# An 8-head edge attention on one core: the tensor engine's semaphores raised by drain instructions instead of by the matmuls

## The chip, the cores and the metric

The kernel runs on one core of a Trainium2 chip. The metric is the device time in microseconds (us) of one execution of the whole program. The engines are called PE (tensor), DVE (vector), ACT (scalar), POOL (GpSimd) and SP (sync, which here only issues DMAs).

## The reference

A two-layer graph transformer over 6,250 nodes of 256 features and 206,250 directed edges sorted by destination. Each layer adds a graph part and a dense mixing part, then a mixture-of-experts part. The change lies in the graph part of the first layer, an 8-head softmax attention over the edges that end in each node:

```
q = (h @ Wq + bq).reshape(n, HD, HEADS) * scaling
k = (h @ Wk + bk).reshape(n, HD, HEADS)
v = (h @ Wv + bv).reshape(n, HD, HEADS)
s = einsum('edh,edh->eh', q[rows], k[cols])
m = segment_max(s, rows)
e = exp(s - m[rows])
z = segment_sum(e, rows)
attn = e / z[rows]
out = segment_sum(attn[:, None, :] * v[cols], rows)
```

Everything else in the two layers (projections, mixing, experts, the second layer's edge sums) is as before and runs in stages of its own, with a barrier between two stages.

## The kernel before, in words

`edge_attention` works on edges in steps of 256: two tiles of 128 edges (one edge to a partition) whose destinations lie in one window of 128 nodes. There are 856 steps (`NSTEP`), taken in chunks of 8 (`CS`), so 107 chunks (`NCH`) of 16 tiles. `chunks` is a hardware loop whose body holds two chunks, one for each of two buffers `s`. All queues are written out by hand, engine by engine, and each engine goes through its list in order; semaphores join them. `at(eng, sem, c, per, i)` waits until `sem` has reached `c * per + i + 1`; with a loop register for the value it issues a register operation (L43), the wait (L45) and a no-op.

What a chunk i needs, in the order of the data:

- POOL gathers key and value rows of the 16 tiles (`gather`, L928, an indirect DMA for each tile) into `kv[:, s]`; each group of four tiles waits for `agg_ps` of chunk i - 2.
- ACT builds one-hot matrices: `oht` (L941, L946) and `oh` (L957, L964).
- PE `expand` (L1033): four matmuls of 128 x 256 for a group of four tiles spread the query rows of the windows over the edges, into one half of `psQ`; the group raises `q_ps`. DVE `product` (L1111) multiplies by the keys, `over_heads` (L1116) reduces to scores.
- PE `turn_scores` (L1040) transposes the scores (`st_ps`); DVE `scans` (L1126 to L1128); PE M1 (L1067, `m1_ps`); DVE `carries` (L1134 to L1137); PE M2 (L1072, `m2_ps`); DVE `maxima` (L1141 to L1150); ACT exponentials (L1002, L1003); PE transposes the weights into `psP` (L1079, `p_ps`); DVE `rescale` (L1155) and PE FAC (L1081, L1082, `fac_ps`); DVE `correct` (L1172) scales the first accumulator row.
- DVE `weigh` (L1165) multiplies the values by the weights, four tiles at a time; PE `sums` adds them up: for each step u two matmuls with the one-hot weights (L1048, L1049) and a third with the identity that adds the accumulator row (L1053), which raises `agg_ps`. ACT `keep` (L968) copies the result back to the accumulator row (`acc_done`). Step u's first matmul waits for `keep` of u - 2 (the half of `psA`), its third for `keep` of u - 1 (the row).

PE's own order in the body for chunk i is: M1; steps 4 and 5 of chunk i - 1; M2; steps 6 and 7 of chunk i - 1; `expand` group 1 of chunk i + 1; the transpose into `psP`; FAC; `expand` group 2; steps 0 and 1 of chunk i; `expand` group 3; steps 2 and 3; `turn_scores` of chunk i + 1; `expand` group 0 of chunk i + 2. `windows` (L885) loads registers with the numbers of the windows, five times a chunk on PE. In the profile each fp32 matmul stands as two records (x2 in the timeline) and so does its weight load; the 128 x 128 transposes are one.

Of the kernel before, what the change touches and what calls it, by code (L numbers as in the profile page):

```python
# [26 lines left out]
P = 128  # L27
N = 6250
C = 256
# [571 lines left out]
def at(eng, sem, c, per, i):  # L601

    v = c * per + i + 1
    if not isinstance(v, int) or v > 0:
        wait_reg(eng, sem, v)
# [214 lines left out]
def edge_attention(nc, k, w):  # L820
# [5 lines left out]
    with ExitStack() as c:  # L826
# [3 lines left out]
        oht = sb("oht", [P, 2, CT * P])  # L830
# [6 lines left out]
        S = sb("S", [P, CT, HEADS])  # L837
        FL = sb("FL", [P, 2 * P])
        F, L = FL[:, 0:P], FL[:, P:2 * P]
        R, E = (sb(n, [P, P]) for n in ("R", "E"))  # L840
        rhs1 = sb("rhs1", [P, 2, CT])
        xs, ys, rhs2 = sb("xs", [HEADS, CT + 1]), sb("ys", [HEADS, CT + 1]), sb("rhs2", [HEADS, 2, CT])
        junk, inr = sb("junk", [P, 2, CT]), sb("inr", [P, 2])
        fd, fx, gm, ohrow = sb("fd", [HEADS, 1]), sb("fx", [HEADS, 1]), sb("gm", [HEADS, HEADS]), sb("ohrow", [HEADS, P])
        psQ = c.enter_context(nc.psum_tensor("e_psQ", [P, 2, 4, C], F32))
        psA = c.enter_context(nc.psum_tensor("e_psA", [P, 2, 512], F32))
        psX = c.enter_context(nc.psum_tensor("e_psX", [P, 512], F32))
        psP = c.enter_context(nc.psum_tensor("e_psP", [P, 512], F32))
        ST, M1, M2, FAC = psX[:, 0:P], psX[0:HEADS, P:P + 2 * CT], psX[:, 2 * P:2 * P + 2 * CT], psX[:, 3 * P:3 * P + HEADS]
# [4 lines left out]
        q_ps, st_ps, m1_ps, m2_ps, p_ps, fac_ps, agg_ps = (sem(n) for n in (  # L854
            "q_ps", "st_ps", "m1_ps", "m2_ps", "p_ps", "fac_ps", "agg_ps"))
# [6 lines left out]
        acc = k.QA  # L862

        def chunks(eng, body):

            body(0, 0)
            body(1, 1)
            with eng.Fori(1, (NCH - 3) // 2) as j:
                body(2 * j, 0)
                body(2 * j + 1, 1)  # L870
            for i in range((NCH - 3) // 2 * 2, NCH):
                body(i, i % 2)

        def first_of(i):
            return isinstance(i, int) and i == 0

        def last_of(i):
            return isinstance(i, int) and i == NCH - 1

        def inside(i):  # L880
            return not isinstance(i, int) or i < NCH

        def windows(engine, first, n, table=k.step_i):

            return nc.values_load_multi_w_load_instructions(  # L885
                table[0:1, bass.ds(first, n)], engines=[engine], min_val=0, max_val=NT + 1 if table is k.step_r else NT - 1,
                skip_runtime_bounds_check_because="the tables hold the window of each step, min(count, NT - 1), or NT + 1")[1]

        @block.sync
        def _(sp):  # L890
            sp.dma_start(acc[:, 1:NT + 1, 0:C], k.Q.rearrange("(t p) c -> p t c", p=P)).then_inc(q_in, 16)

            def ahead(i, s):
                at(sp, oht_abs, i - 2, 2, 1)
                sp.dma_start(relb[:, s, :], k.REL.rearrange("s e -> (s e)")[bass.ds(i * CT * P, CT * P)].partition_broadcast(P))\
                    .then_inc(rel_in[s], 16)

            def behind(i, s):
                at(sp, x3_done, i - 2, 1, 0)
                sp.dma_start(t3[:, s, :], k.T3D[bass.ds(i * CT, CT), :].unsqueeze(1).to_broadcast([CT, HEADS, TW])).then_inc(t3_in[s], 16)  # L900
                sp.dma_start(flg[:, s].rearrange("p t f -> p (t f)"),
                             k.FLG.rearrange("t f -> (t f)")[bass.ds(i * CT * 4, (CT + 1) * 4)].partition_broadcast(HEADS)).then_inc(flg_in[s], 16)
            ahead(0, 0)
            ahead(1, 1)
            behind(0, 0)

            def body(i, s):
                if inside(i + 2):
                    ahead(i + 2, s)
                if inside(i + 1):  # L910
                    behind(i + 1, 1 - s)
            chunks(sp, body)
# [114 lines left out]
        @block.tensor  # L1027
        def _(pe):
            def expand(i, s, g, b):
                at(pe, oht_done, i, 2, g // 2)  # L1030
                at(pe, mul_done, i, 4, g - 2)
                for t in range(4 * g, 4 * g + 4):
                    last = pe.matmul(psQ[:, g % 2, t % 4, :], oht[:, s, t * P:(t + 1) * P],  # L1033
                                     acc[:, bass.ds(b[t // 2 % 4] + 1, 1), 0:C].rearrange("p a n -> p (a n)"), start=True, stop=True)
                last.then_inc(q_ps, 1)

            def turn_scores(i):
                at(pe, s_done, i, 4, 3)
                at(pe, x3_done, i - 1, 1, 0)
                pe.transpose(ST, S[:].rearrange("p t h -> p (t h)"), k.ident[:]).then_inc(st_ps, 1)  # L1040

            def sums(i, s, g, r):
                at(pe, pv_done, i, 4, g)
                if g % 2 == 0:
                    at(pe, oh_done, i, 2, g // 2)
                for u in (2 * g, 2 * g + 1):
                    at(pe, acc_done, i, CS, u - 2)
                    pe.matmul(psA[:, u % 2, 0:VW], oh[:, s, 2 * u, :], kv[:, s, 2 * u, C:KW], start=True, stop=False)  # L1048
                    pe.matmul(psA[:, u % 2, 0:VW], oh[:, s, 2 * u + 1, :], kv[:, s, 2 * u + 1, C:KW], start=False, stop=False)  # L1049
                    at(pe, acc_done, i, CS, u - 1)  # L1050
                    if u == 0:
                        at(pe, fac_done, i, 1, 0)
                    pe.matmul(psA[:, u % 2, 0:VW], k.ident[:], acc[:, bass.ds(r[u % 4], 1), :].rearrange("p a n -> p (a n)"),  # L1053
                              start=False, stop=True).then_inc(agg_ps, 1)
            pe.wait_ge(q_in, 16)
            pe.wait_ge(zeroed, 3)
            for g in range(4):
                if g % 2 == 0:
                    b = windows(mybir.EngineType.PE, 2 * g, 4)
                expand(0, 0, g, b)  # L1060
            turn_scores(0)
            expand(1, 1, 0, windows(mybir.EngineType.PE, CS, 4))

            def body(i, s):
                more = inside(i + 1)
                at(pe, x1_done, i, 1, 0)
                pe.matmul(M1, k.selh[:], rhs1[:].rearrange("p a t -> p (a t)"), start=True, stop=True).then_inc(m1_ps, 1)  # L1067
                if not first_of(i):
                    r = windows(mybir.EngineType.PE, i * CS - 4, 4, k.step_r)
                    sums(i - 1, 1 - s, 2, r)  # L1070
                at(pe, x2_done, i, 1, 0)
                pe.matmul(M2, k.selT[:], rhs2[:].rearrange("p a t -> p (a t)"), start=True, stop=True).then_inc(m2_ps, 1)  # L1072
                if not first_of(i):
                    sums(i - 1, 1 - s, 3, r)
                if more:
                    expand(i + 1, 1 - s, 1, windows(mybir.EngineType.PE, i * CS + CS, 4))
                at(pe, exp_done, i, 1, 0)
                at(pe, pv_done, i - 1, 4, 3)
                pe.transpose(psP[:, 0:P], E[:], k.ident[:]).then_inc(p_ps, 1)  # L1079
                at(pe, g_done, i, 1, 0)  # L1080
                pe.matmul(FAC, k.ones[0:1, :], k.ones[0:1, 0:HEADS], start=True, stop=False)  # L1081
                pe.matmul(FAC, ohrow[:], gm[:], start=False, stop=True).then_inc(fac_ps, 1)  # L1082
                if more:
                    b = windows(mybir.EngineType.PE, i * CS + CS + 4, 4)
                    expand(i + 1, 1 - s, 2, b)
                r = windows(mybir.EngineType.PE, i * CS, 4, k.step_r)
                sums(i, s, 0, r)
                if more:
                    expand(i + 1, 1 - s, 3, b)
                sums(i, s, 1, r)  # L1090
                if more:
                    turn_scores(i + 1)
                if inside(i + 2):
                    expand(i + 2, s, 0, windows(mybir.EngineType.PE, i * CS + 2 * CS, 4))
                if last_of(i):
                    for g in range(2, 4):
                        sums(i, s, g, windows(mybir.EngineType.PE, i * CS + g // 2 * 4, 4, k.step_r))
            chunks(pe, body)

        @block.vector  # L1100
# [2242 lines left out]
```

## Time and profile before

| | us |
|---|---|
| time, median of 3 runs | 9517.41 |
| lowest and highest run | 9510.29, 9522.67 |
| profiled execution, its span (first to last instruction; it is all that is given of this execution's own time) | 11525.6 |
| the edge attention of the change, in the profiled execution | 3305 (600 to 3905 us) |

The profiled execution took 2,008 us more than the median of the timed runs, and nothing tells how this is shared out over the stages. The page gives busy times of engines, the stretch windows give the same for one stage with the granted clock of PE and the busy share of the 16 DMA engines, and the timeline gives instructions with the idle time before them in brackets.

### The profile page before, as it was taken

The page shows a single profiled execution, that of the slowest core. Times are in us where ns is not written, and L with a number is a line of the kernel's source. Part 1 is how long each engine was busy: PE and PEld are TensorE (multiplying, and loading weights), DVE is VectorE, ACT ScalarE, POOL GpSimd, SP SyncE. Part 2 cuts the span into 40 slices and gives each one's busy share as a digit, 9 for nine tenths or more (in the row PEclk, how much of TensorE's full clock was granted, in tenths as well). Part 3 has the DMA queues.
Part 4 walks back from the last instruction along what each step waited for, and adds up shares of the span by engine and source line. Part 5 has one row for each costly group of instructions (what it writes and reads, how often), then busy time and mean ns, then how long its engine had stood idle before and what let it go on. Part 6 is the DMA issues. An engine that isn't in the chain of part 4 may idle for free. (4 is left out here: it accounts for less than half of the span.)

```text
span 11525.6 us, 128623 instructions
## 1 busy us (share of the span) xinstructions
PE 7080.4 (61%) x28206; PEld 5254.5 (46%) x28207; DVE 4671.1 (41%) x10764; ACT 3053.2 (26%) x7326; POOL 5829.5 (51%) x6292
## 2 busy tenths in 40 slices
PE   6757777777777877775777455554444624344342
PEld 3345555555555676665765234333333413223231
DVE  6755566656565565554555111111111302111125
ACT  2244444444444311111111133332222201011010
POOL 1145455545554206666664466666666354545541
PEclk9889999989999987767787666666666767677675
DMA  3255555555555332224444333333223311111114
GB/s 99 85 189 165 161 163 166 163 160 164 162 164 163 117 111 68 66 66 130 140 137 123 91 103 103 104 98 88 85 86 88 97 24 35 29 30 32 29 31 145
DMA packets 656102, 1227.40 MB, mean 106 GB/s; under 512 B 164894, under 2 KB 408018, under 8 KB 655797
## 3 DMA queue, kind: packets, MB, share of 16 engines
q0 software_dynamic: 300272, 718.30, 22.8%
q1 hardware_dynamic: 328103, 467.66, 12.9%
q10 hardware_dynamic: 27580, 39.79, 0.9%
q8 instruction: 54, 0.88, 0.0%
q14 instruction: 93, 0.76, 0.0%
HBM read 1088.28 MB, written 145.05 MB: 107 GB/s over the span
## 5 line engine op out<-in xcount | busy, mean ns | idle before, releaser
L928 POOL DMA_INDIRECT e_kv<-KV,e_idx x1712 | 1622.4, 948 | 987.2 <-issue 483.2
L2454 POOL DMA_INDIRECT s_x<-XN,s_idx x1712 | 1621.5, 947 | 590.0 <-issue 521.6
L1578 POOL DMA_INDIRECT SD<-o_pay,o_pos x1024 | 1074.7, 1050 | 688.7 <-DVEq L45 300.6
L2512 PE MATMUL s_psA<-s_x,s_oh 128*128 128x257 f32 x1712 | 697.8, 497 | 874.7 <-DVE NS L2549 623.3
L2869 POOL DMA_INDIRECT t_g<-G,t_idx x1088 | 1033.5, 950 | 333.7 <-issue 333.7
L2549 DVE TENSOR_TENSOR NS<-s_psA,NS 128x257 f32 x856 | 364.8, 426 | 2021.6 <-DMA hold<-T3D 1309.3
L3047 PE MATMUL t_psY<-t_w,t_H 128*128 128x256 f32 x1600 | 451.5, 450 | 1069.3 <-issue 608.3
L1033 PE MATMUL e_psQ<-QA,e_oht 128*128 x3424 | 890.6, 406 | 194.6 <-issue 178.1
L3047 PEld LDWEIGHTS t_psY<-t_w,t_H 128*128 128x128 f32 x1600 | 363.7, 231 | 1161.0 <-issue 909.7
L2512 PEld LDWEIGHTS s_psA<-s_x,s_oh 128*128 128x128 f32 x1712 | 390.1, 244 | 1072.5 <-issue 991.3
L1053 PE MATMUL e_psA<-QA,ident 128*128 x1712 | 645.1, 463 | 361.3 <-ACT QA L968 220.8
L1033 PEld LDWEIGHTS e_psQ<-QA,e_oht 128*128 128x128 f32 x3424 | 665.0, 202 | 362.4 <-issue 267.7
L968 ACT ACTIVATE QA<-e_psA 128x264 f32 x856 | 332.0, 388 | 1689.7 <-PE e_psA L1053 1237.2
L2988 DVE TENSOR_TENSOR t_y<-t_psY,t_b 128x512 f32<-128x512 f32 x100 | 68.2, 691 | 1614.0 <-DMA X<-s_xb 1186.7
L1048 PE MATMUL e_psA<-e_kv,hold 128*128 128x264 f32 x1712 | 610.5, 442 | 132.2 <-issue 84.0
L2513 PE MATMUL s_psA<-s_x,s_oh 128*128 128x257 f32 x1712 | 652.1, 470 | 0.0
L2473 ACT ACTIVATE s_oh<-iota,s_relt 128x128 f32<-128x128 f32 x1712 | 516.9, 387 | 305.4 <-DMA hold<-T3D 249.5
L1053 PEld LDWEIGHTS e_psA<-QA,ident 128*128 128x128 f32 x1712 | 339.1, 219 | 563.2 <-issue 516.0
L1049 PE MATMUL e_psA<-e_kv,hold 128*128 128x264 f32 x1712 | 586.3, 428 | 0.0
L1165 DVE TENSOR_TENSOR e_kv<-e_psP,e_kv 128x1056 f32<-128x1056 f32 x428 | 533.8, 1248 | 129.0 <-DMA MV<-mixp 102.6
L1111 DVE TENSOR_TENSOR e_kv<-e_psQ,e_kv 128x1024 f32<-128x1024 f32 x428 | 521.5, 1219 | 153.1 <-PE e_psQ L1033 97.1
L957 ACT ACTIVATE hold<-iota,e_relt 128x128 f32<-128x128 f32 x1712 | 542.0, 388 | 18.4 <-issue 9.0
(588 smaller groups left out, 12730.9 us busy)
## 6 DMA issues: line engine op xcount, KB each, us to landing
o_dbf<-DBF SPq DMA_DIRECT2D x128, 512.0 KB
f_w<-in_L_ffn_Wd_dram SPq DMA_DIRECT2D x57, 1024.0 KB
e_relb<-REL SPq DMA_DIRECT2D x107, 512.0 KB
o_dlo<-DLO SPq DMA_DIRECT2D x128, 256.0 KB
e_kv<-KV,e_idx POOLq DMA_INDIRECT x1712
s_x<-XN,s_idx POOLq DMA_INDIRECT x1712
YD<-t_y ACTq DMA_DIRECT2D x50, 512.0 KB
h_yt<-YD SPq DMA_DIRECT2D x10, 2560.0 KB
```

What stands on the lines that cost most here:

```text
L928: pool.indirect_dma_start(kv[:, s, t, :], None, k.KV, bass.IndirectOffsetOnAxis(ap=idx[:, s, t:t + 1], axis=0)).then_inc(kv_in[s][g], 16)
L957: last = act.activation(oh[:, s, t, :], k.iota[:], ACT.Abs, bias=relt[:, s, t:t + 1])
L1033: last = pe.matmul(psQ[:, g % 2, t % 4, :], oht[:, s, t * P:(t + 1) * P], acc[:, bass.ds(b[t // 2 % 4] + 1, 1), 0:C].rearrange("p a n -> p ...
L1048: pe.matmul(psA[:, u % 2, 0:VW], oh[:, s, 2 * u, :], kv[:, s, 2 * u, C:KW], start=True, stop=False)
L1049: pe.matmul(psA[:, u % 2, 0:VW], oh[:, s, 2 * u + 1, :], kv[:, s, 2 * u + 1, C:KW], start=False, stop=False)
L1053: pe.matmul(psA[:, u % 2, 0:VW], k.ident[:], acc[:, bass.ds(r[u % 4], 1), :].rearrange("p a n -> p (a n)"), start=False, stop=True).then_i ...
L1578: pool.indirect_dma_start(self.k.SD, bass.IndirectOffsetOnAxis(ap=self.pos[:, s, j:j + 1], axis=0), self.pay[:, s, j, :], None).then_inc(s ...
L2454: pool.indirect_dma_start(x[:, s, t, 0:C], None, k.XN2, bass.IndirectOffsetOnAxis(ap=idx[:, s, t:t + 1], axis=0)).then_inc(x_in[s], 16)
L2512: pe.matmul(psA[:, u % 4, 0:C + 1], oh[:, o, 2 * u, :], x[:, s, 2 * u, :], start=True, stop=False)
L2513: pe.matmul(psA[:, u % 4, 0:C + 1], oh[:, o, 2 * u + 1, :], x[:, s, 2 * u + 1, :], start=False, stop=True)\
L2869: pool.indirect_dma_start(g[:, s, j, :], None, k.G, bass.IndirectOffsetOnAxis(ap=idx[:, s, j:j + 1], axis=0)).then_inc(g_in[s], 16)
L3047: last = pe.matmul(psY[:, h, b, 0:C], H[:, 4 * e_ + m, i * P:(i + 1) * P], w2[:, 4 * e_ + m, :], start=(m == 0), stop=(m == 3))
```

## The change

In `edge_attention` alone, at seven places, the semaphore increment moves from the last matmul of a group to a `drain` instruction of PE behind it. The matmuls, their order and all waits stay. `drain` makes PE's queue wait until the work issued before it is finished, and then raises the semaphore.

```
             def expand(i, s, g, b):
...
-                    last = pe.matmul(psQ[:, g % 2, t % 4, :], ...
-                last.then_inc(q_ps, 1)
+                    pe.matmul(psQ[:, g % 2, t % 4, :], ...
+                pe.drain().then_inc(q_ps, 1)
...
-                pe.transpose(ST, S[:]..., k.ident[:]).then_inc(st_ps, 1)
+                pe.transpose(ST, S[:]..., k.ident[:])
+                pe.drain().then_inc(st_ps, 1)
...
                     pe.matmul(psA[:, u % 2, 0:VW], k.ident[:], acc[...],
-                              start=False, stop=True).then_inc(agg_ps, 1)
+                              start=False, stop=True)
+                    pe.drain().then_inc(agg_ps, 1)
...
-                pe.matmul(M1, ...).then_inc(m1_ps, 1)
+                pe.matmul(M1, ...)
+                pe.drain().then_inc(m1_ps, 1)
...
-                pe.matmul(M2, ...).then_inc(m2_ps, 1)
+                pe.matmul(M2, ...)
+                pe.drain().then_inc(m2_ps, 1)
...
-                pe.transpose(psP[:, 0:P], E[:], k.ident[:]).then_inc(p_ps, 1)
+                pe.transpose(psP[:, 0:P], E[:], k.ident[:])
+                pe.drain().then_inc(p_ps, 1)
...
-                pe.matmul(FAC, ohrow[:], gm[:], ...).then_inc(fac_ps, 1)
+                pe.matmul(FAC, ohrow[:], gm[:], ...)
+                pe.drain().then_inc(fac_ps, 1)
```

## Rows read from the trace of the kernel before

**Rows 1.** The page: span, and busy time of each engine.

```profile
span 11525.6 us, 128623 instructions
...
PE 7080.4 (61%) x28206; PEld 5254.5 (46%) x28207; DVE 4671.1 (41%) x10764; ACT 3053.2 (26%) x7326; POOL 5829.5 (51%) x6292
```

**Rows 2.** Stretches: length, busy PE, PEld, DVE, ACT, POOL, clock, DMA share, GB/s.

```profile
600.00:3905.00 3305.00, 2539.04 (x9625) 1831.11 (x9626) 1965.32 (x3115) 1545.33 (x3529) 1644.34 (x1824) 0.91 0.55 163
...
4500.00:4750.00 250.00, 185.63 (x901) 156.80 (x900) 140.72 (x487) 31.10 (x66) 159.51 (x152) 0.69 0.24 69
...
2032.00:2034.00 2.00, 2.00 (x10) 1.74 (x10) 1.39 (x6) 1.56 (x3) 1.23 (x2) 1.00 0.00 0
...
2040.50:2044.50 4.00, 1.13 (x4) 0.68 (x4) 0.72 (x2) 0.00 (x0) 1.36 (x2) 0.92 0.94 336
...
2057.50:2061.50 4.00, 2.75 (x12) 1.68 (x10) 0.05 (x1) 0.91 (x1) 1.89 (x2) 1.00 0.76 218
```

**Rows 3.** Groups of instructions from 1500 to 3000 us: busy, mean ns, idle before.

```profile
L928 POOL DMA_INDIRECT e_kv<-KV,e_idx x787 | 746.1, 948 | 460.2 <-issue 220.6 <-PE e_psA L1053 200.2 <-POOL e_idx L925 39.4
...
L1053 PE MATMUL e_psA<-QA,ident 128*128 x789 | 296.8, 462 | 163.1 <-ACT QA L968 97.5 <-DVE QA L1172 61.8 <-issue 3.6
...
L1165 DVE TENSOR_TENSOR e_kv<-e_psP,e_kv 128x1056 f32<-128x1056 f32 x197 | 245.8, 1248 | 61.0 <-DMA MV<-mixp 44.2 <-issue 15.5 <-PE e_psP L1079 1.2
...
L968 ACT ACTIVATE QA<-e_psA 128x264 f32 x395 | 153.2, 388 | 781.9 <-PE e_psA L1053 579.5 <-remote 172.8 <-issue 27.3
```

**Rows 4.** Waits from 1500 to 3000 us: total us, times, longest.

```profile
PE e_psA L1053 <- ACT QA L968: 97.5, 48, 3.4
...
PE e_psA L1053 <- DVE QA L1172: 61.8, 35, 3.6
...
DVE QA L1172 <- DMA MV<-q: 99.5, 41, 4.7
DVE e_xs L1134 <- DMA Q<-qrow: 68.1, 19, 4.4
...
DVE e_kv L1165 <- DMA MV<-mixp: 44.2, 22, 4.1
```

**Rows 5.** Timeline of PE: groups with and without idle time before them.

```profile
2190.82 1.89 PE L1033 MATMUL e_psQ<-QA,e_oht 128*128 x8
2193.09 0.30 PE L1079 MATMUL e_psP<-ident,e_E 128*128 128x128 f32 x1 [0.38 <-issue]
...
2194.38 1.99 PE L1033 MATMUL e_psQ<-QA,e_oht 128*128 x8 [0.46 <-ACT e_oht L946]
...
2197.10 0.61 PE L1053 MATMUL e_psA<-QA,ident 128*128 x2
2197.54 0.61 PE L1048 MATMUL e_psA<-e_kv,hold 128*128 128x264 f32 x2
```

**Rows 6.** Timeline of all engines: three of PE's results and who takes them.

```profile
2031.61 0.40 PE L1072 MATMUL e_psX<-e_rhs,selT 8*128 8x32 f32 x2
...
2032.12 0.19 DVE L1141 TENSOR_TENSOR e_junk<-e_psX,maskj 128x32 f32<-128x32 f32 x1 [0.61 <-PE e_psX L1072]
...
2037.59 0.36 PE L1082 MATMUL e_psX<-e_gm,e_ohrow 8*128 8x8 f32 x2
...
2044.22 0.43 DVE L1172 TENSOR_TENSOR QA<-QA,e_psX 128x264 f32 x1 [3.28 <-DMA MV<-q]
...
2057.37 0.23 PE L1067 MATMUL e_psX<-e_rhs,selh 128*8 128x32 f32 x2
...
2061.45 0.23 DVE L1134 TENSOR_TENSOR_SCAN e_xs<-e_flg,e_xs,e_psX 8x16 f32<-8x16 f32 x1 [4.23 <-DMA Q<-qrow]
```

**Rows 7.** Drains on PE's queue at barriers, with PE's last matmuls before one.

```profile
L826 PEldq DRAIN  x1: 732/732/732, 3905.7 to 3905.7; - x1
...
L128 PEldq DRAIN  x15: 8/13/13, 24.3 to 11525.1; - x15
...
3905.71 0.64 PE L1053 MATMUL e_psA<-QA,ident 128*128 x2
```

More of the change, by code:

```diff
@@ L1032, in expand @@
                 for t in range(4 * g, 4 * g + 4):
-                    last = pe.matmul(psQ[:, g % 2, t % 4, :], oht[:, s, t * P:(t + 1) * P],
-                                     acc[:, bass.ds(b[t // 2 % 4] + 1, 1), 0:C].rearrange("p a n -> p (a n)"), start=True, stop=True)
-                last.then_inc(q_ps, 1)
+                    pe.matmul(psQ[:, g % 2, t % 4, :], oht[:, s, t * P:(t + 1) * P],
+                              acc[:, bass.ds(b[t // 2 % 4] + 1, 1), 0:C].rearrange("p a n -> p (a n)"), start=True, stop=True)
+                pe.drain().then_inc(q_ps, 1)
             def turn_scores(i):
@@ L1039, in turn_scores @@
                 at(pe, x3_done, i - 1, 1, 0)
-                pe.transpose(ST, S[:].rearrange("p t h -> p (t h)"), k.ident[:]).then_inc(st_ps, 1)
+                pe.transpose(ST, S[:].rearrange("p t h -> p (t h)"), k.ident[:])
+                pe.drain().then_inc(st_ps, 1)
             def sums(i, s, g, r):
@@ L1066, in body @@
                 at(pe, x1_done, i, 1, 0)
-                pe.matmul(M1, k.selh[:], rhs1[:].rearrange("p a t -> p (a t)"), start=True, stop=True).then_inc(m1_ps, 1)
+                pe.matmul(M1, k.selh[:], rhs1[:].rearrange("p a t -> p (a t)"), start=True, stop=True)
+                pe.drain().then_inc(m1_ps, 1)
                 if not first_of(i):
@@ L1071, in body @@
                 at(pe, x2_done, i, 1, 0)
-                pe.matmul(M2, k.selT[:], rhs2[:].rearrange("p a t -> p (a t)"), start=True, stop=True).then_inc(m2_ps, 1)
+                pe.matmul(M2, k.selT[:], rhs2[:].rearrange("p a t -> p (a t)"), start=True, stop=True)
+                pe.drain().then_inc(m2_ps, 1)
                 if not first_of(i):
@@ L1078, in body @@
                 at(pe, pv_done, i - 1, 4, 3)
-                pe.transpose(psP[:, 0:P], E[:], k.ident[:]).then_inc(p_ps, 1)
+                pe.transpose(psP[:, 0:P], E[:], k.ident[:])
+                pe.drain().then_inc(p_ps, 1)
                 at(pe, g_done, i, 1, 0)
                 pe.matmul(FAC, k.ones[0:1, :], k.ones[0:1, 0:HEADS], start=True, stop=False)
-                pe.matmul(FAC, ohrow[:], gm[:], start=False, stop=True).then_inc(fac_ps, 1)
+                pe.matmul(FAC, ohrow[:], gm[:], start=False, stop=True)
+                pe.drain().then_inc(fac_ps, 1)
                 if more:
```

## The prediction

> **What bounds the kernel now.** I read the page first. It names no full engine: PE is busy for 61% of the span and the others for less [rows 1]. A change at one stage is worth what that stage makes of it, so the next view is the stretch of the stage: 3,305 us for 107 chunks, which is 30.9 us a chunk, of which PE is busy for 2,539 us or 23.7 us a chunk, against 18.4 on DVE, 15.4 on POOL and 14.4 on ACT. The granted clock is 0.91, that is mostly the 2.4 GHz level with some time at 1.2 [rows 2]. So PE is the fullest engine and leaves 7.2 us a chunk idle. POOL looks idler than it is: its 16 gathers take 0.948 us each and have issue time between them, but its largest outside wait is for the `agg_ps` of PE's L1053 (200 of 460 us of idle time) [rows 3]; it follows PE.
>
> The groups and the waits show what PE's idle time is. From 1500 to 3000 us there are 789 records of L1053, two for each step, eight steps a chunk: 49.3 chunks. L1053 has 163 us of idle time before it, 97.5 for ACT's copy back and 61.8 for DVE's `correct` [rows 3, 4]; together 159 us, 3.2 us a chunk. The rest is short gaps between groups. ACT for its part waits 580 us for L1053 [rows 3]. The stage is a ring in which PE's sums, ACT's copies and DVE's steps hand to one another, with PE the fullest.
>
> The third thing to see is when PE's results are taken. M2 ends at 2032.01 us and DVE starts on it 0.11 us later. FAC ends at 2037.95 and DVE's `correct`, idle for 3.28 us, starts at 2044.22; M1 ends at 2057.60 and DVE, idle for 4.23 us, starts at 2061.45 [rows 6]. The page puts these waits down to DMAs (`MV<-q`, `Q<-qrow`) that this stage doesn't have; the semaphore numbers are used again by other stages. What these DVE instructions wait for is `fac_ps` and `m1_ps` of PE. So in this execution some of PE's semaphores are seen 4 to 6 us after the matmul ended. In the quick case the DMA engines' share is 0.00; in the two late ones it is 0.94 and 0.76 [rows 2]. Over 49.3 chunks the waits of this kind at L1172, L1134 and L1165 are 99.5 + 68.1 + 44.2 = 212 us, 4.3 us a chunk [rows 4].
>
> **The change part by part.** Nothing is removed but the increments on matmuls, and nothing is moved. What is added is 17 drains a chunk: four `expand` groups, the score transpose, M1, M2, the weight transpose, FAC and eight steps; 1,819 in all.
>
> The drain itself is cheap: with nothing in flight it takes 8 to 13 ns. Behind matmuls it lasts until they end: the one at the stage's end was issued at 3905.7 and took 0.732 us, to 3906.4, while the last matmul ended at 3905.71 + 0.64 = 3906.35. So it ends about 0.05 us behind them [rows 7].
>
> The cost is what PE no longer overlaps. L1053 lasts 0.61 us, but the next step's L1048 starts 0.44 us after it: 0.17 us of each matmul's tail lies under the next one [rows 5]. Weights for the next matmul are loaded meanwhile, and a group that starts on an empty PE is longer: the same eight records of L1033 take 1.89 us straight behind others and 1.99 us behind a gap, 0.10 us [rows 5]. Then there are the sequencer's own instructions (register operation, wait, no-op, register loads for the windows), which now run ahead while matmuls are queued and would come after the drain. The trace has no drain inside the loop, so I bound them: below 0, above the gap that the sequencer itself leaves before a group on an empty PE, 0.38 us [rows 5]. Per boundary where PE was kept full: from 0.17 + 0.05 + 0.10 = 0.32 to 0.70 us. I take 0.48, a little under the middle, since a gap left by the sequencer can hold part of the tail already. Where PE already stands empty between two groups, tail and restart are paid now; the drain adds 0.05 to 0.20 us, I take 0.10.
>
> In PE's timeline of one chunk (2176 to 2206 us, of which [rows 5] are five lines) 12 of the 17 boundaries show no gap and 5 a gap of 0.26 to 0.80 us. The sum for a chunk is 12 x 0.48 + 5 x 0.10 = 6.3 us, with ends 12 x 0.32 + 5 x 0.05 = 4.1 and 12 x 0.70 + 5 x 0.20 = 9.4 us.
>
> What hides some of it is PE's waiting for ACT and DVE, 3.2 us a chunk [rows 4]: a step whose third matmul would have waited for the copy back loses nothing while the drain before it runs. Part of that waiting comes from the late semaphores, and the timed runs, 2,008 us shorter than the profiled span, should hold less of it. I let 1.8 us of 3.2 be hidden. That leaves 4.5 us a chunk, x 107 = 481 us. Against the profiled execution that makes 11,526 + 481 = 12,007 us; the median of the runs is 9,517, and as the terms are lengths of engine work I add the same sum there: 9,998, say 10,000 us. If that cover is gone, it is 6.3 x 107 = 674 us.
>
> What is late next: the semaphores go up 0.05 us after the matmul and later by what the group itself was held up. ACT's `keep` (0.388 us [rows 3]) takes each step later, behind it the following step's L1053, and POOL's gathers with `agg_ps`; POOL has its 460 us of idle time as room. No DMA is issued by PE, and no queue is passed over.
>
> **The rivals.**
>
> Late semaphores that drains bring forward (faster). If a matmul's semaphore is really held back in the timed runs as well while more matmuls stream behind it, an emptied PE lets it out. Place: DVE at L1172, L1134 and L1165. Price: up to 4.3 us a chunk of waits gone. PE would then not be the bound, so most of the drains' 6.3 us would fall into its 7.2 us of idle time; at 1.6 us exposed the net is -2.7 us a chunk, -290 us: 9,230 us. It decides from the point where the timed runs hold more lateness than what the drains expose. For it: the waits are there, and PE stands idle itself for want of the following copy. Against it: the lateness goes with the DMA share, not with the length of PE's stream, since PE was busy for only 1.13 of the 4 us in which `correct` waited, so no stream held the semaphore back [rows 2, 6]; and the profiled execution is 2,008 us longer than the timed ones, so something in it delays what the timed runs don't delay, and these late semaphores are a candidate. The Trainium skill's page "PSUM — Partial Sum Buffer", section "Engine vs sequencer instructions", speaks against this rival: an increment attached to the matmul fires when it completes, and a drain waits for the engine to be fully idle. By that rule nothing can be won and the drains' sum stands alone, 9,998; rows 6 show lateness all the same, of which that page says nothing.
>
> Drains in the shade (no change). If the ring of ACT and DVE sets the pace in the timed runs and PE has 6.3 us or more a chunk to spare (it has 7.2 idle here), nothing shows beyond some 0.05 us a handover, about 0.1%: 9,527. Against it: if the stage shrinks with the whole (9,517 / 11,526 = 0.83), a chunk is 25.5 us and PE's 23.7 leave 1.8.
>
> A drain that does not hold PE up, so that the change does nothing: 9,517. The 0.732 us of the one behind matmuls speaks against it [rows 7].
>
> A lower clock (much slower). A PE with a hole behind each group may be granted less. Two stretches side by side: busy for 77% of the stage at 0.91, and for 186 of 250 us, 74%, at 0.69 from 4500 us on [rows 2]. Should the stage fall to 0.70, PE's 23.7 us would become 23.7 x 0.91 / 0.70 = 30.8, 7.1 us a chunk more and 760 us in all; with the drains 10,760. Against it: the timed runs of before are denser than the profiled one, and with 4.5 us more a chunk they would about equal it, at 0.91.
>
> **How the numbers follow.** My forecast (PE pays, partly hidden) has 0.68, and its own range is 9,613 (4.1 - 3.2 = 0.9 us a chunk) to 10,450 (8.7 us, short of the upper end of 9.4). The late semaphores have 0.16, drains in the shade 0.06, drains without effect 0.02, the lower clock 0.08. A difference of 0.2%, about 19 us, is what a measurement of this kernel can tell from no change. Faster 0.16, within it 0.07, slower 0.77; the shade case lies on the border. The range goes from 9,500, which takes in the two cases without effect, to 10,450: left out are the faster case and about half the clock's.
>
> **What the profile afterwards would show.** The drains stand on PE's queue, 17 a chunk, most of them 0.2 to 0.7 us long. L1048 starts about 0.9 us behind L1053 instead of 0.44. L1033 has 1.99 us in every group. PE's busy time in the stage stays near 2,540 us and the stage grows from 3,305 by some 480 us; the other stages stay. If the waits of L1172 and L1134 shrink along with the stage, the semaphore rival is right; if the granted clock falls under 0.8, the last one. I'm wrong if the timed runs give PE far more slack than 1.8 us a chunk, or if the sequencer's work after a drain is near nothing.

## The result, and the profile after

The changed kernel takes 10,560.9 us (median of 4 runs, 10,556.8 to 10,572.5), the kernel before 9,516.1: a ratio of 1.110, with a 95% interval of 1.1086 to 1.1112. It is slower by 1,045 us, 9.8 us a chunk and 0.57 us for each of the 1,819 drains. The direction was forecast, the size of 481 us was not.

The first thing the profile of the changed kernel shows is its span, which agrees with its time to a microsecond (10,560 us); that of before was 2,008 us longer than the timed runs. The kernel before, run again on another chip (e1 below), has a span of 9,509.8 us. The record on which the prediction was built seems to come from a chip on which this kernel is simply slower (inferred; the last section tells from what). All comparisons from here on are with this second record, where lines after L820 are numbered one higher than before.

Page of the changed kernel, span and busy times, for [rows 1]:

```profile
span 10560.3 us, 130442 instructions
...
PE 6806.9 (64%) x28206; PEld 5046.2 (48%) x28207; DVE 4676.5 (44%) x10764; ACT 3062.3 (29%) x7326; POOL 5883.1 (56%) x6292
```

The stage in the changed kernel, for [rows 2] (length, busy PE, PEld, DVE, ACT, POOL, clock, DMA share, GB/s):

```profile
603.00:4259.00 3656.00, 2592.36 (x9630) 1767.52 (x9630) 1965.45 (x3105) 1553.33 (x3531) 1645.48 (x1822) 0.93 0.50 148
```

The same in the second record of the kernel before:

```profile
603.00:3212.00 2609.00, 2312.01 (x9630) 1702.47 (x9630) 1947.04 (x3105) 1546.24 (x3531) 1655.99 (x1822) 0.97 0.69 207
```

The stage grew by 1,047 us, so all of the loss is in it. PE was busy for 21.6 of 24.4 us a chunk, 89%, and is now for 24.2 of 34.2. The busy time of the other engines is the same to 1%. Of the 1,047 us, 280 are longer PE busy time (tails that lie beside nothing, and a clock of 0.93 for 0.97) and 767 are idle PE.

**The clock has to be taken out first.** The granted clock has two levels, 2.4 and 1.2 GHz. In this stage PE stood at the lower one for 123 us before and for 500 us in the changed kernel, and this time differs from run to run of the experiments too (14 to 922 us). So each kernel below is also given by its *chunk at full clock*: from the trace, the time from each of the 17 groups of a chunk to the next, first matmul to first matmul, averaged over 104 chunks at each place in the order, without those that touch a stretch at 1.2 GHz, and added up. Before it is 23.42 us, in the changed kernel 31.92, which is 8.50 us more; times 107 that makes 910 us. The other 135 of the 1,045 us are put down to the lower clock, by difference.

Where the idle time stands is in PE's timeline. The changed kernel, for [rows 5] (start, length, what; the idle time before it in brackets):

```profile
2103.10 1.99 PE L1033 MATMUL e_psQ<-QA,e_oht 128*128 x8 [0.54 <-issue]
2105.52 0.68 PE L1049 MATMUL e_psA<-e_kv,hold 128*128 128x264 f32 x2 [0.43 <-issue]
...
2107.32 0.68 PE L1049 MATMUL e_psA<-e_kv,hold 128*128 128x264 f32 x2 [0.23 <-issue]
...
2109.32 0.30 PE L1040 MATMUL e_psX<-ident,e_S 128*128 128x128 f32 x1 [0.43 <-issue]
2110.78 1.99 PE L1033 MATMUL e_psQ<-QA,e_oht 128*128 x8 [1.16 <-issue]
2113.00 0.22 PE L1069 MATMUL e_psX<-e_rhs,selh 128*8 128x32 f32 x2 [0.23 <-issue]
2114.38 0.68 PE L1049 MATMUL e_psA<-e_kv,hold 128*128 128x264 f32 x2 [1.16 <-issue]
...
2127.66 1.99 PE L1033 MATMUL e_psQ<-QA,e_oht 128*128 x8 [1.13 <-issue]
2130.72 0.68 PE L1049 MATMUL e_psA<-e_kv,hold 128*128 128x264 f32 x2 [1.07 <-issue]
```

The second record of the kernel before:

```profile
2103.64 1.99 PE L1034 MATMUL e_psQ<-QA,e_oht 128*128 x8 [0.40 <-ACT e_oht L947]
2105.47 0.61 PE L1049 MATMUL e_psA<-e_kv,hold 128*128 128x264 f32 x2
...
2106.80 0.61 PE L1049 MATMUL e_psA<-e_kv,hold 128*128 128x264 f32 x2
...
2113.87 0.30 PE L1041 MATMUL e_psX<-ident,e_S 128*128 128x128 f32 x1 [0.72 <-DVE e_S L1117]
2114.92 1.99 PE L1034 MATMUL e_psQ<-QA,e_oht 128*128 x8 [0.75 <-issue]
2116.84 0.23 PE L1068 MATMUL e_psX<-e_rhs,selh 128*8 128x32 f32 x2
2117.14 0.68 PE L1049 MATMUL e_psA<-e_kv,hold 128*128 128x264 f32 x2
```

From one step to the next it is 1.80 us where it was 1.33: 0.47 us more, with only a short gap of 0.23 us. From `expand` group 2 to step 0 it is 3.06 where it was 1.83, 1.23 us more; from M1 to step 4 it is 1.38 where it was 0.30, 1.08 us more. What sets these apart from the first is a register load of `windows` behind the drain. Averaged over the stage at full clock, the five places with such a load grew by 0.41 (ahead of `expand` group 0), 0.69 (group 1), 0.70 (group 2), 1.09 (M1 to step 4) and 1.34 us (group 2 to step 0), 4.23 us together. Eleven others grew by 4.83 us (0.18 to 0.62 each), and one shrank: from step 3 to `turn_scores` by 0.56 us, since PE's wait for DVE there is partly covered now.

Durations (shortest, median, longest, in ns) of drains and loads on PE's queue in the changed kernel, 1500 to 3000 us, for [rows 7]:

```profile
L1035 PEldq DRAIN  x177: 1830/1845/3488, 1500.5 to 2988.9; - x177
...
L1056 PEldq DRAIN  x356: 938/1219/2647, 1504.2 to 2999.2; - x178
...
L885 PEldq TENSOR_LOAD <-step_i x132: 328/332/344, 1511.9 to 2987.9; - x132
```

The drain behind the `expand` group that starts at 2103.10 is issued at 2103.3 and stands for 1.845 us, to the group's end: the sequencer had run ahead and now has to stand. What it did in that time before it now does afterwards, with PE empty. PE's queue in the changed kernel from M1 to step 4, where PE stands idle from 2113.22 to 2114.38: the drain, then the register load, two register operations (L43) and three waits (L45), which start about 0.1 us apart:

```profile
L1070 PEldq DRAIN  x1: 222/222/222, 2113.0 to 2113.0; - x1
...
L885 PEldq TENSOR_LOAD <-step_r x1: 331/331/331, 2113.5 to 2113.5; - x1
...
L43 PEldq ALU_OP  x2: 32/32/32, 2113.9 to 2114.1; - x2
...
L45 PEldq EVENT_SEMAPHORE  x3: 51/51/51, 2114.0 to 2114.3; - x3
```

### The profile page after: what moved, and what is told of

Its sections match the earlier page's. It is cut to its first block and busy times, and to the rows that moved or that the text cites. A ratio compares the mean times of both kernels' runs of the same rounds, so it can differ in the third digit from the quotient of the medians.

```text
span 10560.3 us, 130442 instructions
## 1 busy us (share of the span) xinstructions
PE 6806.9 (64%) x28206; PEld 5046.2 (48%) x28207; DVE 4676.5 (44%) x10764; ACT 3062.3 (29%) x7326; POOL 5883.1 (56%) x6292
## 5 line engine op out<-in xcount | busy, mean ns | idle before, releaser
L2518 PE MATMUL s_psA<-s_x,s_oh 128*128 128x257 f32 x1712 | 667.6, 479 | 1105.7 <-DMA s_x<-XN,s_idx 1017.5
L2875 POOL DMA_INDIRECT t_g<-G,t_idx x1088 | 1076.6, 990 | 329.6 <-issue 329.6
L1033 PE MATMUL e_psQ<-QA,e_oht 128*128 x3424 | 927.8, 418 | 464.3 <-issue 298.4
L3043 PE MATMUL t_psH<-t_xT,t_w 128*128 128x384 f32 (+1 forms) x1088 | 423.0, 555 | 381.7 <-ACT t_H L3020 361.2
L1049 PEld LDWEIGHTS e_psA<-e_kv,hold 128*128 128x128 f32 x1712 | 278.7, 205 | 738.1 <-issue 736.3
L2519 PE MATMUL s_psA<-s_x,s_oh 128*128 128x257 f32 x1712 | 628.1, 454 | 0.0
L1054 PE MATMUL e_psA<-QA,ident 128*128 x1712 | 557.7, 409 | 0.0
L1122 DVE TENSOR_REDUCE e_S<-e_kv 128x32 f32<-128x1024 f32 x428 | 519.9, 1215 | 32.0
L3043 PEld LDWEIGHTS t_psH<-t_xT,t_w 128*128 128x128 f32 x1088 | 238.3, 223 | 562.9 <-issue 360.5
```

The source lines that it names most:

```text
L2518: pe.matmul(psA[:, u % 4, 0:C + 1], oh[:, o, 2 * u, :], x[:, s, 2 * u, :], start=True, stop=False)
L2519: pe.matmul(psA[:, u % 4, 0:C + 1], oh[:, o, 2 * u + 1, :], x[:, s, 2 * u + 1, :], start=False, stop=True)\
L2875: pool.indirect_dma_start(g[:, s, j, :], None, k.G, bass.IndirectOffsetOnAxis(ap=idx[:, s, j:j + 1], axis=0)).then_inc(g_in[s], 16)
L3043: last = pe.matmul(psH[:, m % 2, 0:n * P], w1[:, a, m * P:(m + 1) * P], xT[:, a, 0:n * P], start=(a == 0), stop=(a == KC - 1))
```

## The experiments

All leave the computed values as they are. Each is compared with the kernel before on its own chip. The stage and its clock in each profiled run, worked out as said above:

| run | us more than before | stage, us at 1.2 GHz | chunk at full clock | more, x 107 |
|---|---|---|---|---|
| before (e1) | 0 | 123 | 23.42 | 0 |
| e7, no-ops | 0 | 121 | 23.42 | 0 |
| f3, loads ahead, no drains | -44 | 44 | 23.44 | 2 |
| e3, step drains | 175 | 17 | 25.49 | 221 |
| e4, `expand` drains | 208 | 20 | 25.87 | 262 |
| e5, short groups | 266 | 197 | 25.53 | 226 |
| f1, steps and `expand` | 608 | 14 | 29.66 | 668 |
| e6, drains late | 297 | 16 | 26.62 | 342 |
| e2, plain drains | 933 | 267 | 31.60 | 875 |
| f2, changed, loads ahead | 762 | 315 | 29.92 | 695 |
| changed kernel | 1,045 | 500 | 31.92 | 910 |
| e8, two drains | 1,318 | 922 | 33.50 | 1,079 |

The changed kernel again, f4, has 492 us at 1.2 GHz and a chunk of 31.89 us. The stretch view of the stage shows the same shift of the clock, here for e6, f3 and e8:

```profile
603.00:3502.00 2899.00, 2425.72 (x9630) 1651.04 (x9630) 1953.70 (x3103) 1547.10 (x3531) 1645.13 (x1817) 0.99 0.61 186
...
603.00:3176.00 2573.00, 2286.48 (x9630) 1668.44 (x9630) 1946.42 (x3105) 1547.13 (x3531) 1649.27 (x1822) 0.98 0.71 210
...
603.00:4561.00 3958.00, 2746.28 (x9630) 1855.25 (x9630) 1968.94 (x3103) 1555.12 (x3531) 1651.73 (x1818) 0.88 0.45 136
```

Why the clock is lower in one of them than in another was not tried.

**e1**: the kernel before, one run with a profile; its edit is an assertion at build time.

> The kernel before, with nothing of its work changed, for a second record of its trace. If the late semaphores of PE in the first record belong to that recording, this one has a span near 9,515 us, the edge stage in some 2,615 us (3,660 us of the changed kernel less the 1,045 that were lost), that is 24.4 us a chunk, and DVE takes FAC and M1 within 0.2 us of their end when it is free. If they belong to the kernel, the span is again far above the time and the waits of DVE for FAC and M1 are there again.

9,511.5 us, span 9,509.8, stage 2,609 us. DVE takes M1 0.10 us after its end (2116.84 + 0.23, then 2117.17):

```profile
2117.17 0.24 DVE L1135 TENSOR_TENSOR_SCAN e_xs<-e_flg,e_xs,e_psX 8x16 f32<-8x16 f32 x1 [0.49 <-PE e_psX L1068]
```

So the late semaphores of [rows 6] aren't in the timed runs of before, and the rival built on them had nothing to win. This run alone could not tell a disturbing recording from another chip. What PE waits for another engine in this record (1500 to 3000 us, 63 chunks; total us, times, longest):

```profile
PE e_psX L1041 <- DVE e_S L1117: 53.9, 63, 1.6
...
PE e_psQ L1034 <- ACT e_oht L947: 18.7, 46, 0.4
```

That is 1.15 us a chunk. The waits of the third matmul for ACT and DVE in [rows 4] are gone.

**e2**: drains that raise nothing; the increments stay on the matmuls.

```
                 last.then_inc(q_ps, 1)
+                pe.drain()
```

> The 17 drains of a chunk stay, but the increments stand on the matmuls again; the drains raise nothing. Theory A (PE is the bound, each drain empties it and stops its sequencer from running ahead, about 0.57 us each, all exposed): as slow as the changed kernel, 10,560 us, at most 90 us less (1,819 x 0.05). Theory B (the semaphores come later, and the ring of ACT's copies and POOL's gathers pays): near the kernel before, 9,516 to 9,650.

10,448.5 us against 9,515.7: ratio 1.098 (1.0960 to 1.0997), 933 us more. Theory B falls: with its semaphores on the matmuls the kernel loses nearly as much. Of the 112 us that are missing to 1,045, only 0.32 us a chunk, 34 us or 0.02 us a drain, stand at full clock as the price of raising them at the drain; the changed kernel spends more time at 1.2 GHz (500 for 267 us), and that is the rest.

**e3, e4, e5**: the change in parts: only the steps (8 drains a chunk), only the `expand` groups (4), only the five short groups.

> Drains only behind the third matmul of a step (agg_ps), 8 of the 17 a chunk, 856 in all. Theory A: their share by the count, 856 x 0.47 to 0.57 = 400 to 490 us, so 9,920 to 10,000. Theory B: nearly the whole loss, since the ring goes through agg_ps: above 10,300.

> Drains only behind the expand groups (q_ps), 4 of the 17 a chunk, 428 in all. Theory A: 428 x 0.6 to 0.7 us (register loads of the next group stand behind them) = 257 to 300 us, so 9,770 to 9,820. Theory B: next to nothing, under 9,600, since the products have time.

> Drains only behind the five short groups (score transpose, M1, M2, weight transpose, FAC), 535 in all. If the losses of the three parts add up (theory A, PE as the bound), this one gives what the other two leave of 1,045 us: some 300 to 350 us, 9,820 to 9,870. If the parts hide one another, each part alone costs less than its share and the three sum to less than 1,045.

| drains behind | ratio, interval | us more | per drain |
|---|---|---|---|
| steps (856) | 1.018 (1.0166 to 1.0200) | 175 | 0.20 |
| expand (428) | 1.022 (1.0202 to 1.0236) | 208 | 0.49 |
| short groups (535) | 1.029 (1.0269 to 1.0309) | 266 | 0.50 |

All three came out below what theory A gave them, and their sum is 650 us, not 1,045. The parts don't add up. At full clock they are 221 + 262 + 226 = 709 of 910 us, so about half of the missing 395 us is the clock (e3 and e4 stand almost wholly at 2.4 GHz, the changed kernel doesn't). The other 201 us are cover: PE's wait for DVE ahead of `turn_scores`. From step 3 to `turn_scores` it is 2.56 us before, 2.00 with step drains, 1.52 with `expand` drains, 1.74 with the short ones, and 2.00 with all: each part alone hides 0.56, 1.04 and 0.82 us a chunk there, all together hide 0.56 once. The difference, 1.86 us a chunk or 199 us, is what the parts don't add up to.

**f1** was expected from another model: one reserve R of idle PE that any set uses up once, taken from the times, R = (1,045 - 650) / 2 = 198 us or 1.85 us a chunk. It has steps and `expand` groups together, 12 drains a chunk.

> Again drains behind the steps and the expand groups, to be measured on a chip on which the kernel before takes 9,515 us. One common reserve of PE of about 1.9 us a chunk: 587 us more, 10,100. Each set pays for itself: 384 us more, 9,900. Should the kernel before take 11,528 us again: 484 us more, as e9.

10,126.4 against 9,518.3: 1.064 (1.0623 to 1.0656), 608 us more. Adding up would give 383; the expectation with one reserve was 587 and is off by 21. That it came so near is in part luck, since its R holds the clock as well: at full clock R would be (910 - 709) / 2 = 100 us from the three parts and 668 - 221 - 262 = 185 us from f1, which is not one reserve. What f1 does show is that the parts hide in the same waits.

**e6**: the drains directly ahead of the next group's first matmul, behind its waits and loads.

```
                 at(pe, mul_done, i, 4, g - 2)
+                pe.drain()
                 for t in range(4 * g, 4 * g + 4):
```

> Seventeen drains a chunk again, but each stands directly ahead of the next group's first matmul, behind its waits and register loads; the increments are on the matmuls. PE is still emptied as often, but the sequencer's work for the next group is done while the matmuls run. If the lost run-ahead of the sequencer is a large part of the 0.57 us (waits at 0.1 us each, register loads 0.4 us): 1,819 x 0.32 = 580 us, about 10,100. If emptying PE is all of it: 10,560 as before.

9,811.9 against 9,514.9: 1.031 (1.0295 to 1.0329), 297 us more, lower than either expectation. PE is emptied as often, and this is a third of e2's loss. In its timeline the step follows the `expand` group at 2.09 us (2106.07 to 2108.16), not at 3.06:

```profile
2106.07 1.99 PE L1034 MATMUL e_psQ<-QA,e_oht 128*128 x8 [0.50 <-issue]
2108.16 0.71 PE L1051 MATMUL e_psA<-e_kv,hold 128*128 128x264 f32 x2
```

The sequencer had its waits and loads behind it when PE ran empty. At full clock e6 costs 342 us, 0.19 us a drain with what the waits hide taken off; where nothing hides, a step follows the other at 1.70 us instead of 1.33, 0.37 us for emptying. Between e2 and e6 only the place of the drains differs, and at full clock that is 875 - 342 = 533 us, 0.29 us a drain: the sequencer's work behind it.

**e7**: a no-op in place of each drain.

> A no-op of PE's sequencer in place of each drain, increments on the matmuls: the price of one more instruction in the queue alone. Theory A: nothing that shows, within 0.2% of 9,516, as the sequencer runs ahead of the matmuls. If one more instruction is what costs: a good part of 1,045 us.

9,515.4 against 9,514.9: 1.0001 (0.9992 to 1.0011). One more instruction in the queue costs nothing while the sequencer runs ahead.

**e8**: each drain doubled.

> Each drain of the changed kernel doubled; the second finds PE empty. If the cost is in the emptying, the second costs only its issue, 0.05 to 0.1 us each: 90 to 180 us on top of 10,560. If a drain as such is dear (0.5 us each), another 1,000 us, 11,600.

10,833.3: 1.138 (1.1356 to 1.1403), 277 us above the changed kernel of f4 (on another chip). That would be 0.15 us for each second drain, but e8 stands at 1.2 GHz for 922 us where the changed kernel does for 500. At full clock it is 1.58 us a chunk, 169 us, 0.09 us each (two of the 17 places rest on 17 chunks only), and the gap between two steps says the same, 0.31 us for 0.23:

```profile
2109.49 0.68 PE L1051 MATMUL e_psA<-e_kv,hold 128*128 128x264 f32 x2 [0.31 <-issue]
```

On the queue it stands for 13 ns (the second one behind the score transpose, 1500 to 3000 us):

```profile
L1043 PEldq DRAIN  x41: 13/13/13, 1531.2 to 2995.5; - x41
```

So a drain in an empty engine isn't dear as such, and its 0.08 to 0.09 us are as expected; but its length of 13 ns is not its price, and the time of the whole kernel, 277 us more for 90 to 180 expected, is above what was expected because of the clock.

**f2, f4**: four of the five register loads a chunk moved ahead of the drain, into the group that is running; f4 is the changed kernel beside it.

```
-            def expand(i, s, g, b):
+            def expand(i, s, g, b, load=None):
...
+                loaded_ahead = load() if load else None
                 pe.drain().then_inc(q_ps, 1)
+                return loaded_ahead
```

> Again the changed kernel with four of five register loads moved ahead of the drains. If the sequencer's work behind a drain costs: 300 us less than the changed kernel beside it (f4). If emptying PE is all: the same as f4.

> The changed kernel beside the others on one chip. Where the kernel before takes 9,515 us: 10,560. Where it takes 11,528 us with PE's semaphores late: if drains bring those semaphores forward, less than 1,045 us more; if they don't, 12,570 or above.

f4 10,556.3, ratio 1.109 (1.1076 to 1.1110); f2 10,280.0, ratio 1.080 (1.0780 to 1.0814). Moving 428 loads gives back 276 us. Of these, 2.00 us a chunk stand at full clock, 214 us or 0.50 us a load; the rest goes with less time at 1.2 GHz (315 for 492 us). The gap before `expand` group 0 shrinks from 1.16 to 0.65 us, while the one with the load that was not moved (M1 to step 4) stays at 1.16:

```profile
2120.60 1.99 PE L1033 MATMUL e_psQ<-QA,e_oht 128*128 x8 [0.65 <-issue]
2122.82 0.22 PE L1075 MATMUL e_psX<-e_rhs,selh 128*8 128x32 f32 x2 [0.23 <-issue]
2124.19 0.68 PE L1052 MATMUL e_psA<-e_kv,hold 128*128 128x264 f32 x2 [1.16 <-issue]
```

**f3**: the same move without any drain.

> Again the kernel before with the four loads moved ahead, where its time is 9,515 us: up to 75 us less, 9,440, if the loads are what the gaps ahead of expand groups 0 and 1 hold; no change if the waits end later.

9,474.0 against 9,518.3: 0.995 (0.9936 to 0.9963), 44 us less, and faster than both kernels. But its chunk at full clock is 23.44 us, for 23.42 before. The gap before `expand` group 0 is 0.25 us, where it was 0.75, and PE waits for DVE in other places instead:

```profile
2115.34 0.30 PE L1042 MATMUL e_psX<-ident,e_S 128*128 128x128 f32 x1 [1.05 <-DVE e_S L1122]
2115.89 1.99 PE L1033 MATMUL e_psQ<-QA,e_oht 128*128 x8 [0.25 <-issue]
...
2118.71 0.68 PE L1051 MATMUL e_psA<-e_kv,hold 128*128 128x264 f32 x2 [0.68 <-DVE e_kv L1171]
```

At full clock the two gaps with moved loads give up 0.95 us a chunk, and M1 to step 4, group 2 to step 0 and step 3 to `turn_scores` take 0.92 of it back. The 44 us go with the clock: the stage stood at 1.2 GHz for 44 us instead of 123. Why was not tried.

**e9 to e12** were the first attempt at f1, f2 and f3 and one more pair of parts (e10, `expand` and short groups). They ran on a chip on which the kernel before takes 11,528 us, so the expectations' times say nothing there.

> Drains behind the steps and the expand groups, 12 of 17 a chunk. Alone they cost 175 and 209 us. If PE has one common reserve of about 1.9 us a chunk (203 us) that any set of drains uses up once, the two together cost 175 + 209 + 203 = 587 us: 10,100. If each set pays for itself, 384 us: 9,900.

> Drains behind the expand groups and the five short groups, 9 of 17 a chunk. Alone they cost 209 and 266 us. With one common reserve of 203 us: 678 us, 10,190. If each pays for itself: 475 us, 9,990.

> The changed kernel with four of PE's five register loads a chunk moved ahead of the drain that stood before them, into the group whose matmuls are running. In the changed kernel the gaps with a load in them are 0.94 to 1.16 us long and those with waits alone 0.23 to 0.54. If the sequencer's work behind a drain is what costs, 4 x 0.7 us a chunk come back, 107 x 2.8 = 300 us: 10,260. If emptying PE is the cost, nothing comes back: 10,560.

> The kernel before, without drains, with the same four register loads moved ahead of the waits that stand before them. The gaps before expand groups 0 and 1 (0.75 and 0.33 us in the second record of the kernel before) hold a load; 0.4 us of the first and 0.3 of the second would go: up to 107 x 0.7 = 75 us, 9,440. If the waits around them end later than the loads, no change.

The ratios there are 1.043 (1.0400 to 1.0452), 1.072 (1.0686 to 1.0752), 1.070 (1.0671 to 1.0722) and 1.001 (0.9992 to 1.0024). In microseconds e9 is 484 more where f1 is 608, and e11 802 more where f2 is 762; e10 is 835 more and was not run on another chip, so that pair of parts stays open.

## Why the prediction was right or wrong

- **PE pays, since it is the fullest engine: right.** e2 shows it without moving a semaphore, and e7 that it is not the count of instructions. POOL and ACT only follow: their busy times stayed.
- **0.10 us at the five boundaries that showed a gap: this is the step that failed most.** They are the ones ahead of `expand` group 0, of step 4, of the weight transpose, of `expand` group 2 and of `turn_scores`. The first four grew by 0.41, 1.09, 0.47 and 0.70 us, 2.67 us a chunk where 0.5 was set for all five. A gap was read as a PE that has nothing more to lose; but in front of three of the four stands a register load, and what the sequencer had still done under the last matmuls before the gap is now paid in full.
- **The sequencer's work behind a drain, bounded by 0 and 0.38 us: wrong where a register load stands.** The upper bound came from a gap ahead of the weight transpose, where there is none. From `expand` group 2 to step 0 it grew by 1.34 us, for an upper end of 0.70. Averaged over all drains this work is 0.29 us (e2 against e6); moving a load from behind the drain gives 0.50 us back (f2).
- **0.48 us at a boundary where PE was full: right.** A step to a step grew by 0.47 us at full clock, and the twelve together by 6.39 us for 5.76, since the large and the small ones nearly even out. Emptying alone, put at 0.32, is 0.37 there (e6).
- **1.8 us a chunk hidden: wrong.** The cover was taken from the third matmul's waits for ACT and DVE, and these belong to the slow record; e1 has none of them. What cover there is stands ahead of `turn_scores`, and with all drains it hides 0.56 us.
- **The clock: priced as a rival, at a fall to 0.70, and at nothing in the sum.** In the stage it fell from 0.97 to 0.93, and that is 135 us.
- **Together:** 481 us were forecast. The boundaries came out at 9.06 us a chunk and not at 6.3, inside the upper end of 9.4 (295 us more); 0.56 us were hidden for 1.8 (133 us); the clock took 135 us. That makes 1,044 of the 1,045 us.
- **The profile's 17 drains a chunk "most of them 0.2 to 0.7 us long": wrong.** They last 1.2 and 1.8 us behind steps and `expand` groups. The sequencer reaches the drain while the group is still running; that length is the run-ahead that is lost.
- **The other rivals.** Late semaphores that drains let out: not in the timed runs (e1). Drains in the shade: true for the 0.56 us alone. No effect: no.
- **The argument about the recording** ("something in it delays what the timed runs don't delay") reached the right choice by a wrong reason: as far as e12 shows, it was not the recording but the chip.

## What to carry to other kernels

A drain's price is not its tail. It is what the sequencer would have done under the running group: look at what stands between the drain and the next matmul (waits, register operations, loads) and count that at full length, then take off the engine's waits for others once for the whole set of drains, not once for each. If a flush is needed, issue the next group's waits and loads ahead of it (297 us instead of 933 here). A gap ahead of a group is no sign that a drain there is cheap. And when variants of one kernel are compared by their times, look at the granted clock of the stage first: here it made a second drain look nearly twice as dear as it is, and moved loads look like a gain.

## What the runs showed of the hardware that was not expected

**The same kernel at two speeds.** The kernel before took 9,515 to 9,518 us (medians) in the sessions of e1 to e8 and f1 to f4, and 11,528 us in that of e9 to e12 (17 runs, 11,482 to 11,559), each session on one chip, the slow one seen in a single session. The trace of e12, from that chip, has the waits of [rows 4] again, with the same wrong names (1500 to 3000 us):

```profile
DVE QA L1178 <- DMA MV<-q: 99.1, 41, 4.7
...
DVE e_xs L1140 <- DMA Q<-qrow: 62.9, 19, 4.4
DVE e_kv L1171 <- DMA MV<-mixp: 42.8, 20, 4.1
```

Its span of 11,524.5 us fits that of the first record of before (11,525.6) to about a microsecond; that the first record came from such a chip is inferred from this. Nor do drains let the results out there. In e11 on that chip, PE's transpose into `psP` comes 3.33 us after the `expand` group, and DVE takes its result 1.46 us after its end:

```profile
2106.50 1.99 PE L1033 MATMUL e_psQ<-QA,e_oht 128*128 x8 [0.68 <-DVE e_kv L1125]
...
2111.82 0.45 PE L1091 MATMUL e_psP<-ident,e_E 128*128 128x128 f32 x1 [3.33 <-issue]
...
2113.73 1.26 DVE L1179 TENSOR_TENSOR e_kv<-e_psP,e_kv 128x1056 f32<-128x1056 f32 x1 [4.57 <-PEq L1092]
```

The stretch view of the same kernel has a DMA share of 0.91 there:

```profile
2108.00:2114.00 6.00, 1.11 (x5) 0.47 (x4) 1.43 (x3) 2.50 (x7) 3.04 (x4) 0.77 0.91 258
```

The drain behind that transpose (L1092) has a median of 1,097 ns on that chip, and of 302 ns in f2, the same kernel on a chip of the other kind:

```profile
L1092 PEldq DRAIN  x39: 298/1097/1792, 1536.6 to 2981.2; - x39
...
L1092 PEldq DRAIN  x48: 298/302/307, 1505.3 to 2980.5; - x48
```

So the drain waits there as the semaphore did: what is late is PE's completion as the drain and the other engines see it, and with drains the lateness moves onto PE itself. The Trainium skill's page "PSUM — Partial Sum Buffer", section "Engine vs sequencer instructions", has an increment on a matmul fire when the matmul completes; the trace of e1 agrees (0.10 us), and that of e12 doesn't, with waits of up to 4.7 us for results of PE. Whether it is the chip itself or a state that it was in, why completion is late there, and what the whole change costs there, was not tried.

**A drain on an empty engine** stands for 13 ns on the queue and costs 0.08 to 0.09 us (e8, at full clock).
